# Gate, up and down tiles of a fused RWKV-6 and SwiGLU layer: pairs against singles in two buffers, with the diagonal term, the reciprocal roots and the masking redone

## The reference

```python
xn = layernorm(x)
# branch 1, RWKV-6: five mixes of xn and its shift, r/k/v/g projections, decay w
x5  = tanh((xn + delta*x0_mu) @ x0_w.T)          # 5 groups of 32
mix = einsum(x5, x2_w) + x_bias                  # r, w, k, v, g
w   = -exp(tanh((xn + delta*w_mu) @ w_w1.T) @ w_w2.T + w_b2)
# chunks of 32 positions: state update, inter-chunk and intra-chunk terms
diag = einsum('bhncd,hd,bhncd->bhnc', q, u, k)
o_intra = tril(A, -1) @ v + diag[..., None] * v
on  = groupnorm(o_inter + o_intra) * gn_w + gn_b
s   = (on * silu(g)) @ o_w.T
# branch 2, FFN with int32 weights in -127..127, scale 1/127, hidden 3072
h   = silu(xn @ wg.T) * (xn @ wu.T)
g   = silu(h @ wd.T)
out = x + s * g
```

## Time and profile before

| | us |
|---|---|
| median of 3 runs | 5139.38 (5131.75 to 5212.62) |
| the profiled execution | 5128.56 |
| its span on the slowest core (core 1) | 5127.0 |
| spans of all cores | 5089.8 to 5127.0 |
| TensorE matmul busy | 2288.3 (45%) |
| VectorE busy | 1566.0 (31%) |
| ScalarE busy | 1142.9 (22%), of which 656.9 table loads |
| GpSimd busy | 301.1 (6%) |
| bytes moved by DMA | 257.75 MB, mean 50 GB/s |

### The profile page before, as it was taken

One profiled execution on the slowest core, in us unless ns is written; L12 is line 12 of the kernel. 1 busy time (PEld: TensorE's weight loads), 2 busy tenths in 40 slices (PEclk: granted clock), 3 DMA queues, 4 the chain that ended last, 5 costly groups with the idle time before them and its releaser, 6 DMA issues.

```text
span 5127.0 us, 35871 instructions; the slowest of 8 cores (5089.8 to 5127.0 us)
## 1 busy us (share of the span) xinstructions
PE 2288.3 (45%) x11424; PEld 1019.9 (20%) x11424; DVE 1566.0 (31%) x3580; ACT 1142.9 (22%) x1168; POOL 301.1 (6%) x525
## 2 busy tenths in 40 slices
PE   0356324662246622565316652266432664236632
PEld 0122211221112211222102221122211222112211
DVE  0221452205421054211542215421253213522145
ACT  0112312123211222122311222112221122211231
POOL 0010000100000000000001000010000100001000
PEclk9978556785577755777557875678656886567855
DMA  9433113340222402234023320233202331033310
GB/s 160 70 58 62 33 19 68 58 82 5 45 48 51 82 9 45 46 55 77 9 49 57 62 54 9 56 56 70 41 13 61 59 70 31 12 66 58 66 29 13
DMA packets 88441, 257.75 MB, mean 50 GB/s; under 512 B 10206, under 2 KB 10527, under 8 KB 84639
## 3 DMA queue, kind: packets, MB, share of 16 engines
q0 software_dynamic: 83088, 221.82, 24.8%
q1 hardware_dynamic: 5168, 33.62, 3.0%
HBM read 443.65 MB, written 33.55 MB: 93 GB/s over the span
## 4 chain that ended last, share of the span: by engine, by line
DMA 21%; DVE 20%; issue 17%; PEldq 17%; PEld 8%; ACT 6%; ACTq 3%; POOL 3%; another core or an unknown queue 3%; DVEq 2%; POOLq 0%; SPq 0%
PEldq L307 16%; DMA sb_fu<-w_fu 12%; ACT L146 5%; DVE sb_qg L146 4%; DMA sb_fd<-w_fd 4%; ACTq L151 3%; DMA sb_x<-x 3%; DVE sb_gst L146 3%; DVE sb_z L146 2%; DMA sb_vgo<-w_g 2%; PEld Pab L480 2%; PEld Pab L614 2%; POOL sb_fg L589 2%; PEld Psm L618 2%
## 5 line engine op out<-in xcount | busy, mean ns | idle before, releaser
L146 ACT ACT_TABLE_LOAD x512 | 656.9, 1283 | 3944.0 <-PEq L307 3020.4
L614 PE MATMUL Pab<-sb_xnT,sb_fg 128*128 128x512 bf16 x1536 | 481.9, 471 | 613.3 <-DMA sb_fu<-w_fu 574.1
L146 DVE SCALAR_TENSOR_TENSOR sb_hall<-Psm,sb_scr 128x512 bf16<-128x512 f32 x96 | 66.4, 691 | 1350.4 <-ACTq L151 1350.4
L480 PE MATMUL Pab<-sb_hall,sb_fd 128*128 128x512 bf16 x1536 | 374.6, 408 | 144.4 <-DMA sb_fd<-w_fd 141.6
L614 PEld LDWEIGHTS Pab<-sb_xnT,sb_fg 128*128 128x128 bf16 x1536 | 167.0, 113 | 886.0 <-issue 779.0
L423 PE MATMUL PtrT<-sb_id,sb_xnt 128*128 128x128 bf16 x256 | 32.4, 306 | 508.2 <-DVEq L151 368.9
L146 DVE COPY sb_gff<-PtrT 128x1024 bf16<-128x1024 bf16 x32 | 22.1, 691 | 772.0 <-PEq L307 772.0
L990 PE MATMUL Psm<-sb_ones,sb_qg 128*128 128x1 bf16 x128 | 7.8, 165 | 501.6 <-DVEq L151 501.6
L480 PEld LDWEIGHTS Pab<-sb_hall,sb_fd 128*128 128x128 bf16 x1536 | 157.1, 104 | 357.4 <-issue 205.3
L589 POOL DMA_DIRECT2D sb_fg<-w_fg x192 | 109.1, 568 | 1972.9 <-PEq L307 1968.9
L618 PE MATMUL Psm<-sb_xnT,sb_fu 128*128 128x512 bf16 x768 | 214.8, 430 | 0.0
(11 more groups left out here) (151 smaller groups left out, 3232.5 us busy)
## 6 DMA issues: line engine op xcount, KB each, us to landing
sb_fg<-w_fg POOLq DMA_DIRECT2D x192, 256.0 KB, 5.4
sb_fu<-w_fu POOLq DMA_DIRECT2D x192, 256.0 KB, 6.2
sb_fd<-w_fd POOLq DMA_DIRECT2D x64, 768.0 KB, 9.8
sb_x<-x SPq DMA_DIRECT2D x32, 512.0 KB, 3.4
sb_vgo<-w_v POOLq DMA_DIRECT2D x8, 2048.0 KB, 17.0
sb_vgo<-w_g POOLq DMA_DIRECT2D x8, 2048.0 KB, 15.6
sb_vgo<-w_o POOLq DMA_DIRECT2D x8, 2048.0 KB, 20.9
out<-sb_sg POOLq DMA_DIRECT2D x32, 512.0 KB, 4.8
```

Of the source, the lines that this page charges most:

```text
L146: return fn(*a, **k)
L480: e.matmul(bank, sb_fd[:, j, hc, :], sb_hall[:, hc, :], start=(hc == 0), stop=(hc == NHC - 1), skip_group_check=True)
L614: e.matmul(gb, sb_fg[:, sl, c, :], sb_xnT[:, c, :], start=(c == 0), stop=(c == NC - 1), skip_group_check=True)
```

## The change

- `emit_gu` takes single hidden tiles in two sets of buffers. The load of tile hc waits for the matmuls of hc-2. Even tiles use the PSUM banks `Pa` and `Pb`, odd ones `Psm` and `Pmt`. SiLU works on 512 columns, one multiplication follows. `sb_fg` and `sb_fu` have 2 slots instead of 3.
- `emit_down` takes single output tiles in the same way: the load of tile dc waits for dc-2, and each tile has its own 24 matmuls, SiLU (512 columns), 4 transposes and copy.
- The diagonal term of all four slices is computed ahead of `rA` of slice 0, into `sb_mt` and four sets of columns of `Psm`; `pqk_v` and `pdg_t` leave `rB2`, and `pqg_v` no longer waits for them.
- `rsqrt_newton` goes: VectorE makes a reciprocal, and a new function on ScalarE a square root, in the layer norm (`pln_s2`) and the group norm (`pgn_s2`).
- The four selects of the mask become one over 512 columns.
- `sb_sg` is float32 instead of bf16.

```diff
-def rsqrt_newton(e, var_ap, y_ap, tmp_ap, iters=2):
@@ layer norm; the group norm likewise
-                rsqrt_newton(e, sb_st2[:, 12 + t_:13 + t_],
-                             sb_st2[:, 20 + t_:21 + t_],
-                             sb_st2[:, 16 + t_:17 + t_])
+                e.reciprocal(out=sb_st2[:, 16 + t_:17 + t_],
+                             in_=sb_st2[:, 12 + t_:13 + t_])
                 ev[f"lnv{t_}"] = sig(e, cv)
+            def pln_s2(e, en, t_=t_):
+                en.w(cv, ev[f"lnv{t_}"])
+                e.activation(out=sb_st2[:, 20 + t_:21 + t_],
+                             in_=sb_st2[:, 16 + t_:17 + t_], func=AF.Sqrt)
+                ev[f"lnr{t_}"] = sig(e, cs)
+            on("scalar", pln_s2)
@@ emit_down
-                def pd_ld(e, en, dc0=dc0, pi=pi):
-                    if pi >= 1:
-                        en.w(ct, dnev[pi - 1])
-                    for j in range(2):
-                        e.dma_start(sb_fd[:, j], wdr["w_fd"][dc0 + j],
+                def pd_ld(e, en, dc=dc, par=par):
+                    if dc >= 2:
+                        en.w(ct, dnev[dc - 2])
+                    e.dma_start(sb_fd[:, par], wdr["w_fd"][dc],
...
-                    e.activation(out=sb_scr[:, 0:1024], in_=Pab[:, :],
+                    e.activation(out=gsc_ap, in_=bank[:, 0:512],
                                  func=AF.Silu, bias=0.0, scale=INV127)
@@ emit_gu
-                def pf_ld(e, en, hc0=hc0, pi=pi):
-                    if pi >= 1:
-                        en.w(ct, guev[pi - 1])
-                    for j in range(2):
-                        sl = (hc0 + j) % 3
+                def pf_ld(e, en, hc=hc, par=par):
+                    if hc >= 2:
+                        en.w(ct, guev[hc - 2])
+                    e.dma_start(sb_fg[:, par], wdr["w_fg"][hc],
...
+                    e.dma_start(sb_fu[:, par], wdr["w_fu"][hc],
...
-                        en.w(cv, hev[pi - 1])
-                        en.w(cs, ev[f"silu{pi-1}"])
+                        en.w(cv, hev[hc - 2])
+                        en.w(cs, ev[f"silu{hc-2}"])
...
@@ ahead of rA of slice 0
+        for pts in range(NST):
+            def ppq_v(e, en, pts=pts):
+                if pts == 0:
+                    en.w(cs, st["qk_free"])
...
+                else:
+                    en.w(ct, ev[f"ppd{pts-1}"])
+                e.tensor_tensor(out=sb_mt[:],
+                                in0=sb_q[:, :, pts * 128:(pts + 1) * 128],
+                                in1=sb_k[:, :, pts * 128:(pts + 1) * 128],
+                                op=ALU.mult)
+                e.drain()
+                for h in range(NH):
+                    e.tensor_scalar(out=sb_mt[:, h, :], in0=sb_mt[:, h, :],
+                                    scalar1=sb_u[:, h:h + 1], scalar2=None,
+                                    op0=ALU.mult)
+                ev[f"ppq{pts}"] = sig(e, cv)
+            def ppd_t(e, en, pts=pts):
+                en.w(cv, ev[f"ppq{pts}"])
...
+                for h in range(NH):
+                    e.matmul(Psm[:, 40 + 4 * pts + h:41 + 4 * pts + h],
+                             sb_mt[:, h, :], sb_ones[:],
+                             start=True, stop=True, skip_group_check=True)
@@ rB2: pqk_v and pdg_t removed, and in pqg_v
-            en.w(ct, ev[f"dg{ts_}"])
@@ pmt_v
-            for h in range(NH):
-                e.select(out=sb_mt[:, h, :],
-                         mask=sb_sel[:, h * 128:(h + 1) * 128],
-                         on_true=Pmt[:, h * 128:(h + 1) * 128],
-                         on_false=sb_zero[:], add_drain=True)
+            e.select(out=sb_mt[:].rearrange("p h t -> p (h t)"), mask=sb_sel[:],
+                     on_true=Pmt[:, :], on_false=sb_zero[:], add_drain=True)
@@ buffers
-    sb_sg = A("sb_sg", [128, D], BF16)
+    sb_sg = A("sb_sg", [128, D], F32)
```

More of the change, by code:

```diff
@@ L473, in pd_t @@
                     en.w(cv, hev[-1])
-                    if pi == 0:
-                        en.w(cs, ev[f"silu{NHC//2-1}"])
-                    else:
-                        en.w(cs, ev[f"dns{pi-1}"])
-                    for j, bank in ((0, Pa), (1, Pb)):
-                        for hc in range(NHC):
-                            e.matmul(bank, sb_fd[:, j, hc, :],
-                                     sb_hall[:, hc, :],
-                                     start=(hc == 0), stop=(hc == NHC - 1),
-                                     skip_group_check=True)
+                    if dc < 2:
+                        en.w(cs, ev[f"silu{NHC-1}"])
+                    else:
+                        en.w(cs, ev[f"dns{dc-2}"])
@@ L484, in pd_t, with pd_s @@
+                    bank = Pa if dc % 2 == 0 else Pb
+                    for hc in range(NHC):
+                        e.matmul(bank[:, 0:512], sb_fd[:, par, hc, :],
+                                 sb_hall[:, hc, :],
+                                 start=(hc == 0), stop=(hc == NHC - 1))
                     dnev.append(sig_t(e))
                 on("tensor", pd_t)
-                def pd_s(e, en, pi=pi):
-                    en.w(ct, dnev[pi])
+                def pd_s(e, en, dc=dc):
+                    en.w(ct, dnev[dc])
@@ L510, in pd_t2, with pd_v @@
-                    ev[f"gft{pi}"] = sig_t(e)
+                    for ts2 in range(NST):
+                        e.transpose(Ptr[:, ts2 * 128:(ts2 + 1) * 128],
+                                    gsc_ap[:, ts2 * 128:(ts2 + 1) * 128], sb_id[:])
+                    ev[f"gft{dc}"] = sig_t(e)
                 on("tensor", pd_t2)
-                def pd_v(e, en, dc0=dc0, pi=pi):
-                    en.w(ct, ev[f"gft{pi}"])
+                def pd_v(e, en, dc=dc):
+                    en.w(ct, ev[f"gft{dc}"])
@@ L607, in pf_t @@
                     else:
-                        en.w(cv, hev[pi - 1])
-                        en.w(cs, ev[f"silu{pi-1}"])
-                    for j, gb, ub in ((0, Pa, Psm[:, 0:512]),
-                                      (1, Pb, Pmt[:, 0:512])):
-                        sl = (hc0 + j) % 3
-                        for c in range(NC):
-                            e.matmul(gb, sb_fg[:, sl, c, :], sb_xnT[:, c, :],
-                                     start=(c == 0), stop=(c == NC - 1),
-                                     skip_group_check=True)
-                        for c in range(NC):
-                            e.matmul(ub, sb_fu[:, sl, c, :], sb_xnT[:, c, :],
-                                     start=(c == 0), stop=(c == NC - 1),
-                                     skip_group_check=True)
+                        en.w(cv, hev[hc - 2])
@@ L621, in pf_t @@
+                        en.w(cs, ev[f"silu{hc-2}"])
+                    for c in range(NC):
+                        e.matmul(gbank, sb_fg[:, par, c, :], sb_xnT[:, c, :],
+                                 start=(c == 0), stop=(c == NC - 1))
+                    for c in range(NC):
+                        e.matmul(ubank, sb_fu[:, par, c, :], sb_xnT[:, c, :],
+                                 start=(c == 0), stop=(c == NC - 1))
                     guev.append(sig_t(e))
                 on("tensor", pf_t)
-                def pf_s(e, en, pi=pi):
-                    en.w(ct, guev[pi])
-                    if pi >= 1:
-                        en.w(cv, hev[pi - 1])
-                    e.activation(out=sb_scr[:, 0:1024], in_=Pab[:, :],
+                sh = slice(0, 512) if par == 0 else slice(512, 1024)
```

186 lines of the change are left out of this document (69 added, 117 removed).

## The result

The changed kernel takes 4435.66 us, median of 10 runs, where the kernel before took 5169.76, median of 10 beside it. The ratio of comparable runs is 0.8611, with a 95% interval of 0.8582 to 0.8639: 14% faster. A few executions of every kernel are disturbed (one die at a lower granted clock); ratios leave them out, and where a profile caught one, its stages are not compared. The profiled execution has a span of 4435.1 us against 5127.0, 692 us less, where the sum said 752.

The account below looks back on a forecast made before the run. It took chains of waits, chiefly TensorE's for exposed pair loads, as the bound. 78 + 10 - 1.4 + 4.4 + 3 = 94 us a megatile, 752 off 5127, plus 12: 4387 us; own range 4290 to 4490, with two rivals 4285 to 4580.

Parts of the forecast that it names:

- a block of down over 7 us: Sign of being wrong: a down tile's block, forecast at about 5.3 us, takes over 7 us.
- a loop longer than 10.5 us: Sign of being wrong: two gate and up tiles, forecast every 9.7 us, take longer than 10.5 us.
- Gate and up: Gate and up stage: single tiles hide the loads, 124.7 us a megatile against 202.7, gain 78 us.
- The loop of 9.7 us: Gate and up: one buffer's load, 6.1 us, plus one tile's matmuls, 3.6 us, set the interval of two tiles.
- Down: Down stage: eight tiles of 8.0 us plus two g pieces, 72 us against 88, less 6 for clock: gain 10 us.
- three falls in eight: Down stage: three of the eight new idle gaps drop the clock, each costing 1.9 us, 6 us a megatile.
- down runs cold: Rival: all eight gaps in down drop the clock, 2.8 us each, 16 us a megatile over forecast, 4517 us; chance 0.12.
- The diagonal term: Recurrence: four rounds ahead of slice 0 cost 10.0 us, the slices save 8.6, net +1.4 us a megatile.
- Mask: Recurrence: one select of about 1.2 us replaces four taking 2.46, gain 1.1 in four slices, 4.4 us a megatile.
- Roots: Layer and group norm: reciprocal and ScalarE root take 2.1 us against Newton's 2.5, 0.4 in 8 places, 3 us a megatile.
- The limited clock in dense stretches: Rival: dense matmuls run at clock 0.81, costing 31 us a megatile, 4635 us; chance 0.11.
- The loads come no sooner: Rival: each gate and up tile's load takes 8.6 us instead of 6.1, loop 12.2 us, 4567 us; chance 0.10.

## Why the prediction was right, and where its steps were off

The forecast of 4387 us was 1.1% low, and the time lies within both ranges. The main mechanism, the exposed load of the pairs, is shown. That the total came so close is partly luck: down gave 6.7 us a megatile less than forecast, gate and up 3.3 and the norm 1.7 less, while the recurrence gave 3.8 more for a reason that the sum did not have. One of the prediction's own signs of being wrong came: a block of down over 7 us (7.03). The other, a loop longer than 10.5 us, did not on average (10.3), though 23 of 72 calls were.

- **Gate and up** (78 forecast, 74.7 measured; 70.6 when undone). Right in mechanism; the size was helped by two errors of one sign. The stage before is 207.4 us on average, where the fifth megatile that I read has 202.7, and the stage after is 132.7, where I had 124.7. The loop of 9.7 us is 10.3 on average, 16.1 with a projection instead of 14.9, and the last pair 8.2 instead of 7.6. With a third buffer and no wait for `sb_fu` the three are 9.5, 15.4 and 8.0: this is TensorE's own work, which I had at 9.0 to 9.2 and 14.9, and the load decides by 0.8 us. The Trainium skill's "DMA: Bandwidth & Descriptors", Anatomy of one DMA, gave an estimate of 2.6 us for the load, and with it TensorE's own work would have decided. The row was the better guide: the median from issue to landing of `sb_fu` in the changed kernel is 4.8 us, of `sb_fg` 4.0.
- **Down** (10 forecast, 3.3 measured; 2.3 when undone). The step that failed is the clock's price, "three falls in eight". Not three of eight gaps cost the clock but 48 of 56, six in seven. Four of them in each megatile lie ahead of a tile, 1.7 us each, 6.7 us where I had 6. The two others lie ahead of the pieces of the g projection, which I had put in at the full clock (7.8 us for two): 3.2 us more. The trace before showed it already, though not in the earlier trace rows: behind the first pair's gap of 2.64 us that piece took 5.31 us or more in four of eight megatiles. With 72.6 us when all is warm, where I had 72, the stage is 82.5 us; 82.6 is measured and 78 was forecast. The other 2.1 us of the miss are in the starting point: the 88.0 of the earlier trace rows runs to L869 and so holds the head (1.1 there), and that megatile's down stage is 1.0 above the mean of 85.9. The rival "down runs cold" thus came true in its condition, but at 9.9 us a megatile and not at its 22.
- **The diagonal term** (+10.0 and -8.6 forecast, +9.3 and, undone, 9.3 measured). Right in both halves, and so near zero. The prediction's own terms (three times 2.4 and 1.2) add up to 8.4 and not 8.6.
- **Mask** (4.4 forecast, 9.6 when undone). One select takes 1.06 us, close to "about 1.2 us", and saves 1.4 in each slice and not 1.1. The step that failed is that I priced only the VectorE time that the select takes away. Its shorter wait also keeps TensorE's clock for the matmuls behind it, worth the other 4.0 us, which my sum had not looked for, though the same mechanism stood in my rows for down.
- **Roots** (3 forecast). In the recurrence, undoing roots and selects costs 11.0 and selects alone 9.6, so four roots are worth 1.4 us where I had 1.6; single megatiles of these two kernels lie up to 6 us apart, so this is rough. In the changed kernel the reciprocal, table load and root stand as follows:

```profile
2664.58 0.18 DVE L146 RECIPROCAL sb_gst<-sb_gst 128x4 f32<-128x4 f32 x1
2664.87 1.28 ACT L146 ACT_TABLE_LOAD   x1 [3.97 <-DVEq L151]
2666.16 0.20 ACT L146 ACTIVATE sb_gst<-sb_gst 128x4 f32<-128x4 f32 x1
2666.50 1.94 DVE L146 TENSOR_SCALAR sb_z<-sb_o,sb_gst 128x256 bf16<-128x256 f32 x4 [1.74 <-ACTq L151]
```

  1.92 us from reciprocal to the next step against 2.53, a gain of 0.6 in the timeline. In the norm they brought nothing (69.1 after 69.0) instead of 1.6, and undoing them cost 1.0. The later slices come every 11.2 us instead of 11.6, so the root gives its 0.4 there; but the second slice waits for the x load that w_v delays, and that load lands after 15.3 to 17.4 us where the kernel before has 12.0 to 15.7 (the first megatile left out). Why it became later is not shown.
- **The float32 `sb_sg`** (0 forecast). Right: with bf16 the norm is 69.5 and the recurrence 195.6.
- **The limited clock in dense stretches** did not come in the execution that the forecast is held against: the gate and up stage held 0.99 for 132 us with TensorE busy 85% of it, while all eight cores ran the same program. But it exists. The profiled execution of the kernel with work under the w_g load has it in the second megatile's gate and up stage and not in the last one's:

```profile
720.70:869.40 148.70, 133.04 (x489) 49.89 (x490) 44.66 (x43) 55.94 (x61) 24.70 (x46) 0.82 0.54 87
3861.10:3994.20 133.10, 112.53 (x488) 45.62 (x488) 44.65 (x43) 55.87 (x61) 24.65 (x46) 0.99 0.59 95
```

  The stage is 15.6 us longer at 0.82, close to the 15.4 (7.2 + 6.6 + 1.6) that the rival had priced for it. The Trainium skill's "TensorE: Matmul & The Clock Gate", Part 1, gives 13/16 (0.81) for it, and this trace agrees: eight gate matmuls take 2.26 us there, where they take 1.89 at the full and 3.57 at the lower clock.
- **The loads come no sooner** did not come either: the fourth load of a burst took 6.1 us, and the single tile's two land after 4.0 and 4.8.

What stays open: why the second slice's x load lands later than before the change, what decides which of the gaps in down keep the clock, and why cores of one kernel differ in gate and up.

## What to carry to other kernels

A buffer freed in pairs exposes the whole load; freed one by one, the same loads hide, and that is read from two rows, the landing time and the tile time. When a change leaves a gap of some 2 us on TensorE, price the clock behind the gap as well as the gap: both in the stage that is edited and wherever a shorter VectorE step releases matmuls, and for everything that runs behind it, not only the tiles that were edited. And read a stage in all its repetitions before using it as a starting point: one megatile was 4.7 us off the mean in gate and up. And put the consumer of a tile's result behind the next tile's matmuls: here that was worth more (21 us a megatile in down) than everything else that the change did to down.

## What the runs showed of the chip that I had not expected

- The granted clock falls in idle stretches of 2.2 to 2.5 us far more often than not, with the engine busy for 5.3 us or more before them: the matmuls behind 48 of 56 ran slow (blocks at up to 7.03 and not 5.34 us, pieces at 5.31 and not 3.62). Eight matmuls behind each tile whose result nobody reads made the kernel 1.5% faster.
- Work that needs TensorE for 0.3 us a matmul pays for it too: the four matmuls of the state took 1.06 us behind a wait of 2.96 us, 0.60 behind one of 1.54.
- A 2 MB load from GpSimd's queue stretches a 512 KB load on SyncE's queue from about 8 us to about 16, though they are in different queues; in the later slices it takes some 3.5.
- Root and SiLU each bring a table load of 1283 ns in this kernel: the 704 table loads are 903 us of ScalarE, its costliest group. In gate and up they lie beside the matmuls.
